# Rotary halves of band attention placed by on-chip transfers instead of a second projection

## The chip, the cores and the metric

The kernel runs on one core of one Trainium2 chip. The metric is device time in microseconds (us) of one execution. TensorE (PE) multiplies matrices, VectorE (DVE), ScalarE (ACT) and GpSimd (POOL) work on vectors, and SyncE (SP) issues transfers (DMAs). Each engine works through its own queue in order and waits on semaphores for the others. SBUF is the on-chip memory; PSUM holds the results of TensorE.

## The reference

Sixteen sequences `b` of 256 tokens and 128 features pass four attentions and three kinds of step between them, all with residual additions. Only the first attention ("band") and what touches it are changed. For one sequence it computes, with 16 heads of 64 features:

```
x0 = layernorm(x[b])                       # 256 x 128
q = rope(x0 @ Wq.T + bq)                   # 16 heads x 64; k the same with Wk, bk
v = x0 @ Wv.T + bv
rope(y): y*cos + concat(-y2, y1)*sin       # y1, y2: the two halves (32 each) of a head's 64 features
scores = q k^T / 8, causal with a band of 128 tokens; p = softmax(scores)
x[b] += (p @ v) @ Wo.T + bo
```

After it come a SwiGLU feed-forward with integer weights (ffn0), a causal attention with 16 heads of 8 features, ffn0 again, a chunked attention, a feed-forward with four-bit quantised operands (ffn1), a low-rank attention, and ffn1 again. Since the rows of `p` sum to one, the value bias adds the constant row `bv @ Wo.T + bo` to the output of the band attention, and a similar row to that of the low-rank attention.

## The kernel before

All of `x` stays in SBUF. The work is 80 units: band, causal, chunk, lowrank and end, each for the 16 sequences. A unit's steps are: forward (the feed-forward ahead of its attention: `xn`, `xT`, `low`, `ffn`, `hid`, for ffn1 also `xq`, `quant`), finish (`down`, `res`), operands (`xn`, `xT`, `low`, `qk`, `cast`, `v`, for the small heads also `rope`, `stack`), maxima (`score`, `parts`), back (`nm`, `S`, `V`) and tail (`den`, `rden`, `scale` or `ctx`, `ctxT`, then `out`). Steps of several units are interleaved.

The order on each engine is set by a planner (`make_plan`, `queued`) before the kernel is built. It walks a model of the five engines with a table of step durations (`work`), waits (`needs`), a settling time after a step (`SETTLE`), and a table of head starts for each engine, stage and kind (`LEAD`). It also assigns every PE result to one of three PSUM slots of 1024 floats; a slot is taken again only when the step named by `released_by` has read it.

Band operands: for each of 8 chunks of 128 features (two heads), `qk` fills a slot with four 128x256 products: queries, queries with the two halves of every head swapped, keys, keys swapped. Weights and tokens are each split into two terms, so a product takes three matmuls (`mm_split`) and a chunk twelve. DVE adds the bias and multiplies by cosine or sine (four instructions, L1178), POOL adds the two parts into `band_r` (L906), and ACT makes a bf16 copy `band_rb` (L927) for the scores that give the row maxima. `nm` carries the maxima to PE, `S` recomputes the scores in f32 with the maxima subtracted, ACT takes the exponential, `V` multiplies by the values.

Small attentions go through a `stack` step: SP writes `parts` to a scratch tensor in HBM with six DMAs (L839, L842) and reads it back into `band_r` memory with four (L851). The planner counts 3.2 us of SP for it and 4.0 us until it has landed.

`out` of band and lowrank ends each of its two token tiles with a matmul of one row of ones by the constant row. In the preamble, `band_qk` is loaded and split in two halves `a` and `b`, the second at the end of it (L663, L697, L698).

## Time and profile before

| | |
|---|---|
| median of 3 runs | 2307.32 us (2299.85 to 2311.41) |
| the profiled execution | 2302.39 us, of which 2300.6 us span |
| PE / DVE busy | 1884.8 us (82%) / 1554.9 us (68%) |
| ACT / POOL busy | 801.2 us (35%) / 594.2 us (26%) |
| mean granted PE clock | 0.892 |

"Busy" is time with an instruction in work; a wait is idle time in front of an instruction. The granted clock is a share of full speed: 1.0 is 2.4 GHz and 0.5 is 1.2 GHz. The program reads as stages: preamble to 50 us, band to about 870 us, causal to 1350, chunk to about 1700, low-rank to 2187, and the end.

### The profile page before, as it was taken

The page shows a single profiled execution, that of the slowest core. Times are in us where ns is not written, and L with a number is a line of the kernel's source. Part 1 is how long each engine was busy: PE and PEld are TensorE (multiplying, and loading weights), DVE is VectorE, ACT ScalarE, POOL GpSimd, SP SyncE. Part 2 cuts the span into 40 slices and gives each one's busy share as a digit, 9 for nine tenths or more (in the row PEclk, how much of TensorE's full clock was granted, in tenths as well). Part 3 has the DMA queues.
Part 4 walks back from the last instruction along what each step waited for, and adds up shares of the span by engine and source line. Part 5 has one row for each costly group of instructions (what it writes and reads, how often), then busy time and mean ns, then how long its engine had stood idle before and what let it go on. Part 6 is the DMA issues. An engine that isn't in the chain of part 4 may idle for free. (4 is left out here: it accounts for less than half of the span.)

```text
span 2300.6 us, 51723 instructions
## 1 busy us (share of the span) xinstructions
PE 1884.8 (82%) x21385; PEld 1280.5 (56%) x21385; DVE 1554.9 (68%) x3419; ACT 801.2 (35%) x1298; POOL 594.2 (26%) x561
## 2 busy tenths in 40 slices
PE   3899999999999998788888888787767877778785
PEld 2566666666666656354455456676644544445454
DVE  5745555554545546566666667888888888887874
ACT  0333333333333332243344343433333434344342
POOL 1322222222222202011111111224433434333334
PEclk7999999999999999899999998877778878787786
DMA  4000000000000001222222224333212211122110
GB/s 150 1 1 1 1 1 1 1 1 1 1 2 1 1 1 29 70 49 55 55 66 64 48 62 91 88 98 91 65 45 53 42 42 42 44 63 45 41 32 10
DMA packets 167464, 89.54 MB, mean 39 GB/s; under 512 B 9393, under 2 KB 165810, under 8 KB 166978
## 3 DMA queue, kind: packets, MB, share of 16 engines
q1 hardware_dynamic: 167010, 85.70, 15.7%
q8 instruction: 173, 2.83, 0.5%
q0 software_dynamic: 224, 0.54, 0.1%
q14 instruction: 57, 0.47, 0.1%
HBM read 46.36 MB, written 39.85 MB: 37 GB/s over the span
## 5 line engine op out<-in xcount | busy, mean ns | idle before, releaser
L1252 PE MATMUL slots<-band_r 64*64 64x64 bf16 (+4 forms) x5120 | 420.9, 280 | 108.6 <-DVE nmx L1135 61.6
L1007 ACT ACTIVATE probs<-slots 128x1024 f32<-128x1024 f32 (+1 forms) x416 | 357.4, 891 | 413.0 <-PE slots L1252 409.4
L1135 DVE TENSOR_REDUCE nmx<-slots 128x8 f32<-128x1024 f32 (+2 forms) x352 | 407.6, 1214 | 102.6 <-PE slots L1252 102.3
L1252 PEld LDWEIGHTS slots<-band_r 64*128 64x128 bf16 (+2 forms) x5120 | 201.0, 129 | 311.0 <-issue 138.3
L1178 DVE SCALAR_TENSOR_TENSOR rope_part<-slots,bias_qk,rope_band 128x256 f32<-128x256 f32 x512 | 212.5, 478 | 195.3 <-PE slots L1252 171.1
L1252 PE MATMUL slots<-mask,ident_bf 128*128 128x256 bf16 (+1 forms) x896 | 230.0, 340 | 75.7 <-DMA band_r<-scratch 50.2
L1252 PE MATMUL ctx_ps<-probs,band_va 64*32 64x64 f32 (+4 forms) x5120 | 253.7, 326 | 16.0 <-ACT ctxT L927 10.7
L906 POOL TENSOR_TENSOR band_r<-rope_part 128x512 f32<-128x512 f32 x128 | 164.8, 1287 | 275.4 <-DVE rope_part L1178 275.4
L864 POOL TENSOR_TENSOR rstd<-var_eps,minus_half 128x2 f32<-128x2 f32 x128 | 88.7, 697 | 544.8 <-DVE var_eps L1048 541.5
L1252 PE MATMUL slots<-nmT,pick 64*128 64x256 bf16 (+2 forms) x2560 | 219.6, 244 | 0.1
L1252 PE MATMUL slots<-xT,band_qk 128*128 128x256 f32 x1536 | 201.1, 288 | 7.6 <-DVEq L1184 5.4
L1252 PEld LDWEIGHTS slots<-xT,band_qk 128*128 128x128 f32 x1536 | 190.0, 191 | 18.2 <-DVEq L1184 12.2
L1252 PEld LDWEIGHTS ctx_ps<-probs,band_va 128*32 128x32 f32 (+2 forms) x5120 | 145.8, 124 | 93.3 <-issue 25.7
L911 POOL TENSOR_TENSOR small_d<-rope_part,parts 128x512 f32<-128x512 f32 x48 | 55.6, 1159 | 474.0 <-ACT parts L927 473.9
L1252 PEld LDWEIGHTS slots<-mask,ident_bf 128*128 128x128 bf16 x896 | 54.5, 98 | 165.3 <-issue 109.3
L927 ACT ACTIVATE ctxT<-ctx_ps 128x512 f32<-128x512 f32 (+1 forms) x112 | 87.5, 781 | 153.0 <-PE ctx_ps L1252 153.0
L927 ACT ACTIVATE band_rb<-band_r 128x512 bf16<-128x512 f32 x128 | 79.4, 630 | 158.8 <-POOL band_r L906 158.8
L1102 DVE SCALAR_TENSOR_TENSOR rope_part<-band_va,slots 128x352 f32<-128x352 f32 (+2 forms) x128 | 68.4, 535 | 62.2 <-ACT band_va L943 30.9
L1252 PEld LDWEIGHTS slots<-nmT,pick 64*128 64x128 bf16 (+1 forms) x2560 | 103.0, 108 | 9.9 <-issue 2.2
L927 ACT ACTIVATE band_va<-slots 128x256 f32<-128x256 f32 (+1 forms) x80 | 50.7, 637 | 133.7 <-PE slots L1252 133.6
L613 POOL TENSOR_TENSOR band_rb<-band_rb 128x704 f32<-128x704 f32 x32 | 53.9, 1686 | 166.5 <-DVEq L1113 166.5
L1527 PE MATMUL slots<-ident,ctxT 128*128 128x128 f32 x384 | 65.2, 301 | 31.1 <-ACT probs L1007 8.4
(171 smaller groups left out, 2871.4 us busy)
## 6 DMA issues: line engine op xcount, KB each, us to landing
band_r<-scratch SPq DMA_DIRECT2D x192, 192.0 KB
scratch<-parts SPq DMA_DIRECT2D x96, 192.0 KB, 2.2
scratch<-parts SPq DMA_DIRECT2D x96, 128.0 KB, 2.1
scratch<-parts SPq DMA_DIRECT2D x96, 64.0 KB, 1.8
x<-in_x SPq DMA_DIRECT2D x16, 128.0 KB, 2.6
out<-x SPq DMA_DIRECT2D x16, 128.0 KB, 1.8
band_r<-in_band_qk_a SPq DMA_DIRECT2D x1, 1024.0 KB, 6.4
band_r<-in_band_qk_b SPq DMA_DIRECT2D x1, 1024.0 KB, 8.1
```

The source lines that it names most:

```text
L613: lambda: v.tensor_tensor(qx, qx, qp, ALU.add),
L864: nc.gpsimd.tensor_tensor(rstd[:, b], var_eps[:, b], minus_half[:], ALU.pow).then_inc(rstd_ready, 1)
L906: nc.gpsimd.tensor_tensor(band_r[:, b % RING, j], part[:, 0], part[:, 1], ALU.add).then_inc(band_sum, 1)
L911: nc.gpsimd.tensor_tensor(small_d[:], small_r, parts[:, 0], ALU.subtract).then_inc(rest1, 1)
L927: return nc.scalar.activation(dst, src, ACT.Copy)
L1007: nc.scalar.activation(probs[:, g % 2, step[2], :, 0:width], slot(u, step).rearrange("p (a n) -> p a n", a=2)[:, :, 0:width], ACT.Exp, sca ...
L1102: link(nc.vector.scalar_tensor_tensor(g_out, t_in, 1.0, gate, ALU.add, ALU.mult))
L1135: nc.vector.tensor_reduce(dst, src, axis=AX.X, op=ALU.max, negate=True).then_inc(free_sem(u, step), 1)
L1178: nc.vector.scalar_tensor_tensor(rope_part[:, c % 2, rot, qk, :], slot(u, step)[:, o:o + TOK], bias_qk[:, j, 2 * qk + rot:2 * qk + rot + 1 ...
L1252: return nc.tensor.matmul(o, lhsT, rhs, start=start, stop=stop, skip_group_check=shared)
L1527: last = nc.tensor.transpose(B[:, g * P:(g + 1) * P], ctxT[:, g, t * P:(t + 1) * P], ident[:])
```

## The change

1. Band weights are regrouped. A fill now holds four heads (a "quad"): first halves of queries and keys, then second halves, four heads of 32 features on the 128 partitions. There are 4 fills for each sequence instead of 8, and nothing is projected twice.
2. DVE still runs 32 multiplications for a sequence: step `qk` makes the first rotated half (first half by cosine, second by sine), step `rot` the second. A slot is held until `rot` is done. POOL subtracts or adds into a new buffer `quad_r` (two quads deep).
3. SP then copies `quad_r` into `band_r` with four transfers of 32 partitions x 512 floats (64 KB) after `qk` and four after `rot`: 32 for a sequence. ACT waits for them (`band_moved`) and casts two chunks at a time (4 casts of 128x1024 instead of 8 of 128x512).
4. The constants of band and lowrank are added to `x` by POOL (step `bias`, 128x256, 32 times), and the two matmuls in `out` go. `out` on DVE waits for `bias`.
5. The preamble loads and splits `band_qk` once at half the total size, and spreads the two constant rows over 128 partitions with two matmuls and two copies.
6. The planner's numbers change: `stack` 7.6 us of SP and 4.3 us to land, settling times for SP by step, all head starts, and the term for the unit's number. So the order changes in every stage.

```
-        for j in range(CHUNKS + CAST_LAG):
-            if j < CHUNKS:
-                steps.append(("qk", j))
-            if j >= CAST_LAG:
-                steps.append(("cast", j - CAST_LAG))
+        for m in range(QUADS + CAST_LAG):
+            if m < QUADS:
+                steps += [("qk", m), ("rot", m)]
+            if m >= CAST_LAG:
+                steps.append(("cast", m - CAST_LAG))
...
-        "stack": [("sp", 3.2)],
+        "stack": [("sp", 7.6)],
...
-SETTLE = {"pe": 0.18, "act": 0.12, "dve": 0.1, "pool": 0.08, "sp": 4.0}
+SETTLE = {"pe": 0.18, "act": 0.12, "dve": 0.1, "pool": 0.08}
+LANDS = {"stack": 4.3, "qk": 1.7, "rot": 1.7, "res": 1.4}
...
-        "operands": {"band": 19.904, "causal": 0.469, "chunk": 0.14, "lowrank": 3.336},
+        "operands": {"band": 0.166, "causal": -0.064, "chunk": 3.447, "lowrank": 12.532},
...
+    if name == "qk":
+        return u, ("rope",) if small else ("rot", step[1]), "dve"
...
+                    if kind == "band" and step[0] in ("qk", "rot"):
+                        m, second = step[1], step[0] == "rot"
+                        quad = b * QUADS + m
+                        sp.wait_ge(band_sum, 2 * quad + second + 1)
+                        if b >= RING and step == ("qk", 0):
+                            sp.wait_ge(back_full, last_exp(u - RING) + 1)
+                        for i in range(4):
+                            to = 64 * (i % 2) + 32 * second
+                            sp.dma_start(band_r[to:to + 32, b % RING, 2 * m + i // 2],
+                                         quad_r[32 * i:32 * i + 32, quad % 2, second]).then_inc(band_moved[quad % 2], 16)
...
+                    if step == ("bias",):
+                        pool.wait_ge(xn_ready, XN_NO[u, False] + 1)
+                        nc.gpsimd.tensor_tensor(x[:, b], x[:, b], const[kind][:].unsqueeze(1).to_broadcast([P, TILES, DIM]),
+                                                ALU.add).then_inc(const_added, 1)
...
+                        quad, second = b * QUADS + step[1], step[0] == "rot"
+                        n = 2 * quad + second
                         pool.wait_ge(part_ready, 4 * (n + 1))
-                        if b >= RING and j == 0:
-                            pool.wait_ge(back_full, last_exp(u - RING) + 1)
+                        if quad >= 2:
+                            pool.wait_ge(band_moved[quad % 2], 128 * (quad // 2))
...
-                        act.wait_ge(band_sum, b * CHUNKS + j + 1)
+                        act.wait_ge(band_moved[quad % 2], 128 * (quad // 2 + 1))
...
-                            if has_const:
-                                last = mm(o, ones[:], const_row[kind][:], False, True)
```

The order on DVE, in the middle of the band stage, for one sequence. Before, all eight chunks stand together (`rope_part`), after `out` of an earlier sequence:

```order
L1230 TENSOR_TENSOR ctxT<-slots,ctxT 128x512 x4
L1242 TENSOR_TENSOR x<-slots,x 128x256
L1045 BN_STATS stats<-x 128x6 x2
L1047 BN_AGGR mean_var<-stats 128x2 x2
L1048 TENSOR_SCALAR var_eps<-mean_var 128x2
L1178 SCALAR_TENSOR_TENSOR rope_part<-slots,bias_qk,rope_band 128x256 x32
```

The same place now: three quads (24 multiplications), then `qk` and `rot` of the fourth between the maxima (`nmx`) of the sequence before and the `scale` steps (`ctxT`):

```order
L1215 SCALAR_TENSOR_TENSOR rope_part<-slots,bias_qk,rope_band 128x256 x24
L1171 TENSOR_REDUCE nmx<-slots 128x2x4 x2
L1215 SCALAR_TENSOR_TENSOR rope_part<-slots,bias_qk,rope_band 128x256 x4
L1171 TENSOR_REDUCE nmx<-slots 128x2x2
L1261 RECIPROCAL rden<-slots 128x2x4x4
...
L1268 TENSOR_TENSOR ctxT<-slots,ctxT 128x512 x4
L1171 TENSOR_REDUCE nmx<-slots 128x2x2
L1215 SCALAR_TENSOR_TENSOR rope_part<-slots,bias_qk,rope_band 128x256 x4
L1171 TENSOR_REDUCE nmx<-slots 128x2x2
```

So the fourth quad's slot is held through most of the pass over the maxima.

The order on ACT at the start of a back half, before: the copy of the maxima (`nmT`) follows the copies of the values (`band_va`) and `xT`, and the casts (`band_rb`) are spread among the copies of `ctxT`:

```order
L927 ACTIVATE band_rb<-band_r 128x512 x5
L927 ACTIVATE ctxT<-ctx_ps 128x512
L927 ACTIVATE band_rb<-band_r 128x512 x2
L927 ACTIVATE ctxT<-ctx_ps 128x512
L927 ACTIVATE den_sb<-ctx_ps 128x256
L927 ACTIVATE band_rb<-band_r 128x512
L927 ACTIVATE band_va<-slots 128x1024 x2
L927 ACTIVATE xT<-slots 128x256
L927 ACTIVATE nmT<-slots 128x256
```

And now, with all four casts right ahead of `nmT`, which stands behind the last transfer of the fourth quad:

```order
L962 ACTIVATE ctxT<-ctx_ps 128x512 x2
L962 ACTIVATE den_sb<-ctx_ps 128x256
L962 ACTIVATE rdT<-slots 128x256
L962 ACTIVATE band_rb<-band_r 128x1024 x4
L962 ACTIVATE nmT<-slots 128x256
L962 ACTIVATE band_va<-slots 128x1024 x2
L1043 ACTIVATE probs<-slots 128x1024
```

The order on PE in the causal stage. The projection `xT,causal_qkv` feeds the stack of its sequence; the rows `mask` and `band_r 128x128 x8` begin the pass over the maxima. Before, the projection comes after that pass, and its own scores follow a little less than one period later:

```order
L1252 MATMUL slots<-mask,ident_bf 128x512 x2
L1252 MATMUL slots<-band_r 128x128 x8
L1252 MATMUL slots<-mask,ident_bf 128x512 x2
L1252 MATMUL slots<-band_r 128x128 x8
L1252 MATMUL slots<-mask,ident_bf 128x2x128 x2
L1252 MATMUL slots<-band_r 128x256 x4
...
L1252 MATMUL slots<-xT,causal_qkv 128x256 x12
L1252 MATMUL slots<-mask,ident_bf 128x2x128 x2
L1252 MATMUL slots<-band_r 128x256 x2
```

Now it comes ahead of the pass of the sequence before it, so that its own scores follow more than one period later:

```order
L1292 MATMUL slots<-xT,causal_qkv 128x256 x12
L1292 MATMUL slots<-mask,ident_bf 128x256 x2
...
L1567 MATMUL slots<-ident,ctxT 128x128 x4
L1292 MATMUL slots<-mask,ident_bf 128x512 x2
L1292 MATMUL slots<-band_r 128x128 x8
L1292 MATMUL slots<-mask,ident_bf 128x512 x2
L1292 MATMUL slots<-band_r 128x128 x8
```

The projection moved from behind the pass to ahead of it.

## Rows read from the trace of the kernel before

**Rows 1.** Windows by stage: length, busy us per engine, granted clock, DMA.
```profile
112.00:870.00 758.00, 711.13 (x6524) 485.38 (x6520) 404.31 (x935) 245.51 (x382) 164.41 (x141) 1.00 0.01 1
1003.00:1350.00 347.00, 286.97 (x3027) 171.29 (x3026) 226.47 (x492) 132.00 (x223) 44.95 (x51) 0.92 0.24 56
...
1723.00:2187.00 464.00, 353.64 (x3120) 225.54 (x3120) 389.21 (x792) 186.83 (x290) 178.54 (x167) 0.81 0.21 47
2187.00:2301.00 114.00, 78.23 (x624) 55.55 (x622) 70.53 (x156) 37.93 (x61) 45.78 (x39) 0.75 0.08 18
```
**Rows 2.** Timeline of PE over one band sequence: start, us.
```profile
407.53 0.29 PE L1485 MATMUL slots<-ident_bf,nm 128*128 128x128 bf16 x2
...
416.80 0.48 PE L1252 MATMUL slots<-const_band,ones 1*128 1x128 f32 x2
...
422.98 0.61 PE L1252 MATMUL slots<-mask,ident_bf 128*128 128x512 bf16 x2
...
425.94 1.52 PE L1252 MATMUL ctx_ps<-probs,band_va 128*64 128x256 f32 x16
...
431.13 9.02 PE L1252 MATMUL slots<-xT,band_qk 128*128 128x256 f32 x72
...
442.21 1.70 PE L1252 MATMUL slots<-xT,band_qk 128*128 128x256 f32 x12 [0.18 <-DVEq L1184]
443.84 1.52 PE L1252 MATMUL ctx_ps<-probs,band_va 128*64 128x256 f32 x16
...
459.19 0.28 PE L1485 MATMUL slots<-ident_bf,nm 128*128 128x128 bf16 x2
```
**Rows 3.** Timeline of DVE over the same sequence.
```profile
400.07 6.88 DVE L1135 TENSOR_REDUCE nmx<-slots 128x8 f32<-128x1024 f32 x6 [0.99 <-PE slots L1252]
...
411.65 2.48 DVE L1230 TENSOR_TENSOR ctxT<-slots,ctxT 128x512 f32<-128x512 f32 x4 [1.71 <-PE slots L1252]
...
432.94 1.66 DVE L1178 SCALAR_TENSOR_TENSOR rope_part<-slots,bias_qk,rope_band 128x256 f32<-128x256 f32 x4 [11.51 <-PE slots L1252]
434.81 1.66 DVE L1178 SCALAR_TENSOR_TENSOR rope_part<-slots,bias_qk,rope_band 128x256 f32<-128x256 f32 x4 [0.21 <-DVE rope_part L1178]
...
450.01 0.73 DVE L1061 TENSOR_SCALAR xn<-x,mean_var,rstd 128x128 f32<-128x128 f32 x2 [0.89 <-POOL rstd L864]
```
**Rows 4.** Page, costliest groups: line, operation, count, busy, mean ns, idle before.
```profile
L906 POOL TENSOR_TENSOR band_r<-rope_part 128x512 f32<-128x512 f32 x128 | 164.8, 1287 | 275.4 <-DVE rope_part L1178 275.4
```
**Rows 5.** Timeline of SP's queue in the causal stage.
```profile
1038.19 2.52 SPq L851 DMA_DIRECT2D band_r<-scratch  x4
```
**Rows 6.** Page, DMA issues: count, size each, us to landing.
```profile
scratch<-parts SPq DMA_DIRECT2D x96, 64.0 KB, 1.8
```
**Rows 7.** Waits of PE in 860:1000, 1000:1340, 1340:1590: total, times, longest.
```profile
PE slots L1252 <- DMA band_r<-scratch: 10.7, 3, 4.9
...
PE slots L1252 <- DMA band_r<-scratch: 39.5, 12, 4.3
...
PE slots L1252 <- DMA band_r<-scratch: 4.3, 2, 2.6
```
**Rows 8.** Timeline of PE at one of these waits.
```profile
1044.95 0.62 PE L1252 MATMUL slots<-mask,ident_bf 128*128 128x512 bf16 x2 [4.05 <-DMA band_r<-scratch]
```
**Rows 9.** Windows of 2 us around it: length, PE busy, granted clock, DMA.
```profile
1042.00:1044.00 2.00, 0.00 (x0) 1.00 0.88 137
...
1046.00:1048.00 2.00, 2.00 (x15) 0.50 0.00 0
```
**Rows 10.** Timeline of DVE at the end of the preamble.
```profile
36.91 1.23 DVE L697 CAST band_qk<-band_r 128x2048 fp32r<-128x2048 f32 x1
38.17 2.29 DVE L698 TENSOR_TENSOR band_qk<-band_r,band_qk 128x2048 fp32r<-128x2048 f32 x1
```
**Rows 11.** Timeline of POOL in the last 30 us.
```profile
2270.86 1.68 POOL L613 TENSOR_TENSOR band_rb<-band_rb 128x704 f32<-128x704 f32 x1 [2.75 <-DVEq L1113]
...
2285.98 1.67 POOL L613 TENSOR_TENSOR band_rb<-band_rb 128x704 f32<-128x704 f32 x1 [10.21 <-DVEq L1113]
```

More of the change, by code:

```diff
@@ L40 @@
 QUANT_OPS = (range(0, 3), range(3, 6), range(6, 9))
+QUADS = HEADS // 4
 CAST_LAG = 2
@@ L220, in needs @@
             yield u - 1, ("nm",), "pe"
+        if name == "out" and kind in CONSTANT:
+            yield u, ("bias",), "pool"
     if eng == "act":
@@ L242, in needs @@
     if eng == "pool":
+        if name == "bias":
+            yield u, ("xn", False), "dve"
         if step == ("xq", 1):
@@ L308, in released_by, with settles @@
+        "forward": {"lowrank": -1.38, "end": -7.778},
+        "operands": {"band": -33.144, "causal": -56.912, "chunk": 76.381, "lowrank": -16.786},
+    },
+}
+PER_UNIT = 0.0038
+def settles(step, eng):
+    return LANDS[step[0]] if eng == "sp" else SETTLE[eng]
 def released_by(u, step):
```

174 lines of the change are left out of this document (90 added, 84 removed).

## The prediction

> **What bounds the kernel now.** I read the windows by stage first [rows 1]. In the band stage (112 to 870 us) PE is busy 711 of 758 us, 93.8%, at full clock; DVE works 53% of it. So there PE's work is the time, and what leaves PE there pays. In the causal stage PE is busy 83% and DVE 65%, and the mean clock is 0.92: neither fills it. In the low-rank stage DVE is busy 389 of 464 us, 84%, and leads. In the last 114 us both are low (PE 69%, DVE 62%).
>
> The timeline of PE then gives the band period: `nm` to `nm` is 459.19 - 407.53 = 51.66 us [rows 2]. The eight `qk` fills stand together from 431.13 to 443.84, 12.71 us, with two 0.18 us waits for DVE among them [rows 2].
>
> The waits of PE show what the causal stage lacks: 10.7 + 39.5 + 4.3 = 54.5 us in 17 waits for `band_r<-scratch`, the read-back of `stack`, almost one for each causal sequence [rows 7]. One of them, 4.05 us [rows 8], leaves PE without work in 1042 to 1044; the granted clock is 1.00 up to there and 0.50 (1.2 GHz) in 1046 to 1048, while PE is busy throughout [rows 9]. So such a wait costs more than its own length.
>
> **Part 1: projection.** Half of the 96 matmuls go: 12.71 / 2 = 6.36 us for a sequence [rows 2]. The two constant matmuls go too, each 0.48 us [rows 2] with some overlap: 0.9. On a path held by PE that leaves 51.66 - 6.36 - 0.9 = 44.4 us, waits of before included. PE's idle share was 6.2%, or 3.2 us, so PE's own work is then about 51.66 - 3.2 - 6.2 (the 6.36 less one of the two waits) - 0.9 = 41.3; the walk below adds 40.5 of named steps.
>
> **Part 2: the new band order.** DVE's work is unchanged (32 multiplications), but a slot is now held until `rot`, and the fourth quad's is held through the pass over the maxima. I walk one sequence, in us.
>
> First part, from the first score fill to `nm`. PE's own work is 15.5: six scores at about 0.86, one `V` 2.24 (I take `S` at 1.8 wide and 1.1 narrow from the same rows: a wide and a narrow `S` fill 422.98 to 425.94, 2.96 [rows 2]), `out` 4.0, small fills 0.9, two `v` 3.2. DVE has to do, in order: two maxima at 6.88 / 6 = 1.15, `qk` 1.87 (434.81 - 432.94), one maximum, `den` 1.2, one maximum, four `scale` 2.48, one maximum, `rot` 1.87, the last maximum, `parts` 0.9 [rows 3]. That is 15.2, beginning 0.9 after PE. With two free slots only, `scale` waits for DVE's chain: fills for the last two scores come at 10.3 and, behind `out`, at 15.2. `v` is done at 19.3, so `nm` starts at 19.3: 3.8 of wait.
>
> Second part. DVE still has `out` with its statistics (1.7), the statistics of the next sequence (1.3), POOL's root (0.9 of wait) and `xn` 0.73 [rows 3], so `xT` on PE can't start before 3.5 after `nm`; PE meanwhile has `nm` and one wide `S`, 2.0, and a wait of 0.5 for ACT. Three `qk` fills take all slots; the next `S` waits 0.5 for the first `rot`. Together 2.2 of wait on 25.0 of work. Sum: 19.3 + 27.2 = 46.5.
>
> The transfers end in the same place. The fourth `rot` leaves DVE at 14.3; POOL's addition takes 1.29 [rows 4]; four transfers are issued in 2.5 (four take 2.52 [rows 5]); the last lands 1.8 later (64 KB [rows 6]): 19.9, and the cast ends at about 21. `nm`'s copy on ACT is queued behind it, with both `v` copies and the exponentials behind that, so `S` starts 1.2 later; most of this lies in the wait for `xT`, and 0.2 is left. I take **46.7**: 51.66 - 46.7 = 5.0 for each of 16 sequences, **-80 us**. Bounds: no added wait at all (44.4) gives -116; for the transfers the nearest other row is the stack's read-back, whose scores begin 4.2 us after its last issue (1044.95 against 1038.19 + 2.52 [rows 5, 8]), 2.4 more than I used, which gives 49.1 and -41. SP issues 32 x 0.63 = 20 us for a sequence, under half of the period, so the queue keeps up if transfers overlap.
>
> The row for a 64 KB transfer is 1.8 us, between HBM and 128 partitions [rows 6]; none shows 32 partitions. The Trainium skill (SBUF — State Buffer, "Door 1: The DMA port swizzle") says that partitions 0 to 31 reach 8 of the 16 ports, at about 218 GB/s against 436, and advises 128 partitions and large transfers. By it 64 KB cost 0.15 us more, an estimate, and the period would be 46.8. No run here shows this, and neither figure changes the sum.
>
> **Part 3: `bias`.** 32 additions on POOL of half the size of its band addition, 1.29 / 2 = 0.65 us each [rows 4]. POOL is busy 22% in the band stage [rows 1] and the result is wanted by `out`, tens of us later: 0. If POOL held up the first rotated quad, it would be 0.65 x 16 = 10; the removed matmuls in low-rank (0.9 x 16 = 14 on PE) lie beside DVE, which leads there: 0, at best -14.
>
> **Part 4: preamble.** The second split, 1.23 + 2.29 = 3.5 us [rows 10], stands last there and goes. The constant's spreading overlaps the quantised weights' work: **-3.5**, between -3.5 and -1.
>
> **Part 5: the order of the later stages.** Work stays the same but all head starts differ. In the causal stage the projection moves ahead of the previous sequence's pass, so the distance to its own scores grows from less than a period to more than one. It gains at least the pass it is moved past and itself, 6 x 0.86 + 1.6 = 6.8 us; the waits are at most 4.9 [rows 7]. They should go: **-54.5**. Who is late next: PE, or DVE at 65%. The window holds twelve sequences (it runs from the first DMA of one stack to that of the twelfth after it), 28.9 us each, of which PE idles 5.0 [rows 1]; 39.5 / 12 = 3.3 of these are the waits. Bounds: the waits only change name, 0; or they take the half-clock stretches with them: 8% of 347 us is lost to the clock [rows 1], another -28, plus -29 at the end, where five instead of seven ffn1 quantisations are left behind the last low-rank cast, 15.1 us apart (2285.98 - 2270.86 [rows 11]). I leave both out: 6 more feed-forwards now run around the end of band and cost time there, and the ffn1 work moved into the chunk stage fills it.
>
> The Trainium skill (TensorE: Matmul & The Clock Gate, "HAM oscillation — how this bites in real kernels") says that a matmul burst after a DMA wait starts at half clock each time. The trace agrees: 0.50 after 4.05 us [rows 8, 9]. It would speak for the lower bound.
>
> **Sum.** The profiled execution took 2302.4 us (span 2300.6), 4.9 less than the median of 2307.3. 2302.4 - 80 - 3.5 - 54.5 = **2164 us**.
>
> **Rivals.**
> - *Band pays, later stages don't.* DVE or PE takes over the 54.5 us of waits, or the earlier feed-forwards cost them back. For it: DVE already leads in low-rank, 84% [rows 1]. Against: 35% of idle on DVE in causal. 2302.4 - 83.5 = 2219.
> - *Band pays less.* The casts hold ACT, and with it `nm` and `S`, by 2.4 more, as worked out: 2164 + 39 = 2203. The same size results if the 4 us or so without steady work around `nm` brings the half clock for 5 us of each sequence: 2.5 x 16 = 40. Against: 6% of idle left the clock at 1.00 in band before [rows 1].
> - *More than forecast.* The half-clock stretches and the end as above: 2164 - 28 - 29 = 2107.
> - *Slower: the moves run one behind the other.* If a transfer between partitions doesn't overlap the next, a sequence needs 32 x 1.8 = 58 us of them [rows 6] against a period of 51.66; with the later gains that is 2302.4 + 16 x 6 - 58 = 2340. It decides from 2302.4 + 16(32t - 51.66) - 58 = 2302, a transfer time t of 1.73 us. Against: four read-backs of 192 KB, three times the size, are there 1044.95 - 1038.19 = 6.8 us after the first issue [rows 5, 8], less than four times 1.8 in a row.
>
> **How the numbers follow.** Forecast 0.52, of itself 2125 to 2195; band alone 0.14; band less 0.11; more 0.16; slower 0.04; no change, by several smaller losses, 0.03. The range of 2095 to 2225 takes in the three rivals around the forecast. Below 0.5% (about 11 us) a time can't be told from no change here. Faster is 0.93, same 0.03, slower 0.04.
>
> **What would show it.** Band period: 46 to 48 us from `nm` to `nm`, 48 projections in each, PE busy about 88% and still at clock 1.0. Waits of PE for DVE's `nmx` or `xT` near `nm`, and for ACT's `nmT`. Transfers `band_r<-quad_r`: 512, landing near 2 us, issued about 0.6 apart. No or few waits of PE for `band_r<-scratch`, and a causal period under 27 us instead of 28.9. Wrong would be: transfers landing after 4 us or more, clock below 0.95 in band, or a span from the last band exponential to the end as long as before (about 1430 us).

## The result

The changed kernel takes 2299.3 us (median of 20, 2291.8 to 2308.9) against 2306.0 for the kernel before on the same chip (20 runs, 2295.9 to 2317.2): a ratio of 0.9969, interval 0.9954 to 0.9984. The forecast was 2164. A gain of 7 us is left of 138.

The profiled execution takes 2297.8 us, its span is 2295.9. PE is busy 1795.3 us instead of 1884.8. That is 90 us less, where the prediction takes 16 x 7.26 = 116 out of band alone; part of what is left ran at half clock. DVE is busy 1609.8 instead of 1554.9, with no less and no more to compute. The windows by stage of the changed kernel, answering to [rows 1] (its low-rank stage begins later):

```profile
112.00:870.00 758.00, 647.05 (x5796) 412.59 (x5795) 414.53 (x932) 235.26 (x330) 170.22 (x152) 0.91 0.16 40
1003.00:1350.00 347.00, 314.29 (x3436) 191.90 (x3435) 250.71 (x558) 147.97 (x248) 50.65 (x56) 0.98 0.24 62
1774.00:2187.00 413.00, 313.81 (x3040) 210.50 (x3040) 361.38 (x661) 183.46 (x275) 149.57 (x143) 0.86 0.22 56
2187.00:2295.00 108.00, 64.75 (x548) 46.84 (x544) 71.75 (x131) 32.70 (x50) 31.86 (x29) 0.74 0.06 14
```

In the band window PE is busy 64 us less, but its clock is 0.91 where it was 1.00. To see where the time went I cut every trace at the same marks, the starts of the `nm` fills on PE (u is a band sequence, "causal" runs from the `nm` of its first sequence to that of chunk's first). The two left columns add up to the two spans; the others are kernels of the experiments. The period repeats within 0.01 us and the first two rows within 0.6 in two kernels with the same band (deep4 and pool_twice, below). The later rows are less sure: the profiled execution of deep4 is 12 us below that kernel's median, that of bias_only 7 above, and chunk reads 385.8, 387.9 and 391.7 in three kernels with the same order there. A difference of a few us in these rows says nothing.

| us | before | changed | before_late | bias_only | deep4 | pairs | qk2_s31 |
|---|---|---|---|---|---|---|---|
| to `nm` of u0 | 104.1 | 105.3 | 104.0 | 104.1 | 103.4 | 96.6 | 96.5 |
| u0 to u1 | 45.1 | 60.6 | 45.1 | 45.1 | 60.7 | 55.4 | 54.7 |
| u1 to u14, each of 13 | 51.66 | 50.88 | 51.66 | 50.49 | 48.61 | 48.60 | 47.79 |
| u14 to u15 | 28.8 | 32.2 | 28.8 | 27.7 | 32.3 | 32.3 | 32.3 |
| u15 to causal | 77.4 | 107.6 | 104.4 | 72.6 | 107.2 | 107.3 | 107.5 |
| causal | 454.1 | 413.5 | 418.4 | 461.2 | 412.7 | 412.7 | 412.8 |
| chunk | 329.0 | 391.7 | 399.8 | 342.1 | 385.8 | 387.9 | 391.7 |
| low-rank | 525.6 | 463.4 | 483.2 | 526.4 | 458.4 | 461.7 | 461.5 |
| last `nm` to the end | 65.0 | 60.1 | 60.4 | 63.2 | 59.2 | 59.2 | 59.1 |

So the start lost 15.5 us, 13 periods gained 10.1 where 64.5 were forecast (13 x 4.96), and all behind band gained 11.4 net (1479.9 to 1468.5 from the `nm` of u14 on, 3.4 of loss in u14 to u15 included).

The 13 periods in one window each, before, changed and deep4 (the changed kernel with two buffers more, below):

```profile
149.19:820.74 671.55, 630.70 (x5771) 430.72 (x5771) 365.00 (x839) 217.40 (x338) 151.28 (x129) 1.00 0.01 1
165.90:827.40 661.50, 569.46 (x5097) 365.21 (x5096) 372.74 (x846) 205.57 (x287) 159.33 (x143) 0.92 0.17 42
164.14:796.03 631.89, 561.11 (x5097) 363.31 (x5096) 363.04 (x846) 205.37 (x287) 159.80 (x143) 0.95 0.18 44
```

For each period PE is busy 48.5, 43.8 and 43.2 us and idle 3.1, 7.1 and 5.4. The forecast of 46.7 was 41.3 of work and 5.4 of idle. So the changed kernel has 2.5 us more of work than forecast, on a clock of 0.92, and 1.7 more of idle.

**One band sequence after.** The timeline of PE, around the place that [rows 2] show:

```profile
397.99 0.61 PE L1292 MATMUL slots<-mask,ident_bf 128*128 128x512 bf16 x2
...
406.26 1.03 PE L1292 MATMUL slots<-mask,ident_bf 128*128 128x512 bf16 x2 [2.74 <-DVE nmx L1171]
408.59 0.37 PE L1525 MATMUL slots<-ident_bf,rd 128*128 128x128 bf16 x2 [0.76 <-DVE rd L1182]
...
413.42 4.87 PE L1292 MATMUL slots<-band_o,ctxT 128*128 128x128 f32 x32
...
421.87 0.29 PE L1525 MATMUL slots<-ident_bf,nm 128*128 128x128 bf16 x2
...
449.69 0.61 PE L1292 MATMUL slots<-mask,ident_bf 128*128 128x512 bf16 x2
```

From the first score fill (397.99) to `nm` are 23.9 us, where the walk had 19.3; from `nm` to the next first score fill 27.8, where it had 27.2. The loss is in the first part. Follow the 2.74 us back: DVE's maximum was late because the `qk` step of the fourth quad ahead of it had waited for POOL, and POOL had waited for a transfer. POOL, DVE and SP's queue at that time:

```profile
386.00 1.27 POOL L940 TENSOR_TENSOR quad_r<-rope_part 128x512 f32<-128x512 f32 x1 [0.29 <-DVE rope_part L1215]
402.11 2.49 POOL L940 TENSOR_TENSOR quad_r<-rope_part 128x512 f32<-128x512 f32 x2 [14.85 <-DMA band_r<-quad_r]
406.64 1.26 POOL L940 TENSOR_TENSOR quad_r<-rope_part 128x512 f32<-128x512 f32 x1 [2.04 <-DMA band_r<-quad_r]
```
```profile
403.42 1.66 DVE L1215 SCALAR_TENSOR_TENSOR rope_part<-slots,bias_qk,rope_band 128x256 f32<-128x256 f32 x4 [2.10 <-POOL quad_r L940]
...
406.73 1.22 DVE L1180 TENSOR_TENSOR nmx_r<-rden,rd 128x32 f32<-128x32 f32 x1
```
```profile
394.27 7.06 SPq L858 DMA_DIRECT2D band_r<-quad_r  x10
```

The transfer itself is quick to land, as the page's part on DMA has it (answering to [rows 6]):

```profile
band_r<-quad_r SPq DMA_DIRECT2D x512, 64.0 KB, 2.0
```

What held it is what SP waited for between 200 and 750 us (total, times, longest):

```profile
SPq L855 <- PE slots L1292: 261.7, 10, 26.9
```

L855 is SP's wait for the last `S` of the sequence two before: `band_r` has two entries, and the first quad's transfers overwrite the one which that `S` still reads. The new order puts three `qk` fills of u ahead of `S:1,1` to `S:3,1` of u - 2. Their sums come in 380.99 to 387.27, `quad_r` holds two quads, and nothing leaves until 394.27. Then the sixteen transfers of these two quads are issued in a row, 0.7 us each.

The windows of 2 us show the second price. PE has no work in 404 to 406, and then runs at 1.2 GHz for 10 us:

```profile
404.00:406.00 2.00, 0.00 (x0) 0.00 (x0) 2.00 (x4) 0.00 (x0) 0.61 (x1) 0.84 0.45 113
406.00:408.00 2.00, 1.57 (x6) 0.26 (x6) 1.90 (x5) 0.00 (x0) 1.26 (x1) 0.50 0.40 101
...
412.00:414.00 2.00, 2.00 (x8) 0.76 (x9) 0.92 (x2) 0.00 (x0) 0.00 (x0) 0.50 0.39 98
414.00:416.00 2.00, 2.00 (x13) 2.00 (x13) 2.00 (x5) 0.00 (x0) 0.00 (x0) 0.60 0.00 0
```

`band_o` takes 4.87 us here; at full clock its two groups take 2.05 each.

### The profile page after: what moved, and what is told of

Read it like the earlier page. It is cut to its first block and busy times, and to the rows that moved or that the text cites. A ratio compares the mean times of both kernels' runs of the same rounds, so it can differ in the third digit from the quotient of the medians.

```text
span 2295.9 us, 50383 instructions
## 1 busy us (share of the span) xinstructions
PE 1795.3 (78%) x20493; PEld 1228.5 (54%) x20493; DVE 1609.8 (70%) x3419; ACT 787.6 (34%) x1234; POOL 615.8 (27%) x593
## 5 line engine op out<-in xcount | busy, mean ns | idle before, releaser
L1171 DVE TENSOR_REDUCE nmx<-slots 128x8 f32<-128x1024 f32 (+2 forms) x352 | 415.3, 1217 | 235.6 <-PE slots L1292 231.3
L1292 PE MATMUL slots<-band_r 64*64 64x64 bf16 (+4 forms) x5120 | 400.6, 272 | 93.1 <-DVE band_r L1139 44.2
L940 POOL TENSOR_TENSOR quad_r<-rope_part 128x512 f32<-128x512 f32 x128 | 162.3, 1274 | 490.3 <-DVE rope_part L1215 246.6
L1292 PE MATMUL ctx_ps<-probs,band_va 64*32 64x64 f32 (+4 forms) x5120 | 262.6, 327 | 27.3 <-issue 16.4
L1215 DVE SCALAR_TENSOR_TENSOR rope_part<-slots,bias_qk,rope_band 128x256 f32<-128x256 f32 x512 | 207.6, 476 | 66.7 <-PE slots L1292 37.5
L1292 PEld LDWEIGHTS ctx_ps<-probs,band_va 128*32 128x32 f32 (+2 forms) x5120 | 148.3, 125 | 107.8 <-issue 58.1
L962 ACT ACTIVATE band_rb<-band_r 128x1024 bf16<-128x1024 f32 x64 | 63.0, 1047 | 195.4 <-PE slots L1292 140.1
L1292 PE MATMUL slots<-xT,band_qk 128*128 128x256 f32 x768 | 103.3, 292 | 3.8 <-DVE xT L1114 3.7
L1292 PEld LDWEIGHTS slots<-xT,band_qk 128*128 128x128 f32 x768 | 96.9, 194 | 11.3 <-issue 9.7
L1097 DVE TENSOR_SCALAR band_va<-x,mean_var,rstd 128x128 f32<-128x128 f32 x128 | 91.7, 717 | 6.4 <-POOL rstd L894 1.7
L1292 PE MATMUL slots<-fp_gu,xTf 128*128 128x352 f32 x384 | 75.1, 348 | 17.3 <-DVE xTf L1114 16.9
L1081 DVE BATCH_NORM_STATS2 stats<-x 128x6 f32<-128x128 f32 x256 | 75.2, 294 | 13.1 <-DMA x<-in_x 4.6
```

The source lines that it names most:

```text
L940: nc.gpsimd.tensor_tensor(quad_r[:, quad % 2, second], part[:, 0], part[:, 1], ALU.add if second else ALU.subtract).then_inc(band_sum, 1)
L962: return nc.scalar.activation(dst, src, ACT.Copy)
L1081: link(nc.vector.bn_stats(stats6[:, t, :], x[:, b, t, :]))
L1097: last = nc.vector.tensor_scalar(xn[:, t, :], x[:, b, t, :], mean_var[:, b, t, 0:1], rstd[:, b, t:t + 1], ALU.subtract, ALU.mult)
L1171: nc.vector.tensor_reduce(dst, src, axis=AX.X, op=ALU.max, negate=True).then_inc(free_sem(u, step), 1)
L1215: nc.vector.scalar_tensor_tensor(rope_part[:, c % 2, sine, qk, :], slot(u, ("qk", m))[:, at * TOK:(at + 1) * TOK], bias_qk[:, m, at:at + 1 ...
```

## The experiments

All ratios are to the kernel before, which ran beside each.

### Is it the wait for `band_r`?

**deep4**: four rotated sums may lie waiting, not two; the order is untouched.

```diff
-        quad_r = sb("quad_r", [P, 2, 2, 2, TOK])
+        quad_r = sb("quad_r", [P, QBUF, 2, 2, TOK])      # QBUF = 4, as the band_moved semaphores
-                        if quad >= 2:
-                            pool.wait_ge(band_moved[quad % 2], 128 * (quad // 2))
+                        if quad >= QBUF:
+                            pool.wait_ge(band_moved[quad % QBUF], 128 * (quad // QBUF))
```

> The changed kernel with four rotated-sum buffers (quad_r) instead of two; the order of the work is the same. Theory (the ring wait): in the changed kernel the transfers of a sequence's first quad wait on SP's queue for the last S of the sequence two before, whose copy of band_r they overwrite; two quads of sums fill quad_r, GpSimd then waits 14.9 us for a transfer, DVE 2.1 us and TensorE 2.7 us behind it, and the granted clock is 0.50 for the next 9 us. With four buffers GpSimd's wait goes below 2 us, the clock of that place is back near 1.00, the row max nmx_r beside the add is near 0.2 us again instead of 1.22, and the band's period falls from 50.9 us to 46.5 to 48; 14 periods of 3 to 4.4 us are 40 to 60 us: 2240 to 2258 us, 0.972 to 0.980 of the kernel before. Rival one (the clock and the waits come from the order of the fills, not from the buffers): period 50 to 51, 2290 to 2300 us. Rival two (the wait only moves to the casts on ACT, since band_r is still two sequences deep): GpSimd is free, but a TensorE wait for the cast of 2 us or more appears and the period is 49 to 50: 2272 to 2285 us.

Measured: 0.982 (0.979 to 0.985), 2265.9 us, 34 less than the changed kernel. POOL waits for no transfer any more, SP waits as before (286.5 us in 11 waits), and `nmx_r` takes 0.19. The wait is shown to be the cause of 2.3 us a period, 30 of the 34. But the period is 48.6, not 46.5 to 48, and the time lies between the theory's range and that of its second rival. From `nm` (406.92) to the first score fill (434.74) are 27.8 us, as before; the rest is 21.7, and the half clock is still in it, later. (The period shown is one of the long ones, 49.5.) PE's timeline and one window of 2 us of deep4:

```profile
439.86 0.41 PE L1547 MATMUL slots<-ident,den_sb 128*128 128x128 f32 x2 [0.22 <-ACT den_sb L963]
440.96 0.61 PE L1293 MATMUL slots<-mask,ident_bf 128*128 128x512 bf16 x2 [0.69 <-DVE nmx L1172]
...
446.87 6.00 PE L1293 MATMUL slots<-band_o,ctxT 128*128 128x128 f32 x32
...
456.46 0.29 PE L1526 MATMUL slots<-ident_bf,nm 128*128 128x128 bf16 x2
```
```profile
440.00:442.00 2.00, 1.20 (x8) 0.26 (x7) 1.86 (x6) 0.00 (x0) 0.98 (x1) 1.00 0.39 98
```

The granted clock puts a price on it. Six of deep4's 13 periods hold 6.8 us at 1.2 GHz and take 49.2 us on average, the other seven hold 3.4 us and take 48.1: 1.0 us for 3.4 us of half clock.

**late_qk**: the same wait removed by order; the planner gets back the rule of the kernel before.

```diff
+        if kind == "band" and step == ("qk", 0) and u >= RING:
+            yield u - RING, LAST_S["band"], "pe"
```

> The changed kernel with one rule added to the order's planner, the one that the kernel before had: the first fill of a sequence's quads stands behind the last S of the sequence two before on TensorE. The buffers are as in the changed kernel. Theory (the ring wait): SP's wait for band_r before the first quad's transfers is then over when they are issued, GpSimd's 14.9 us wait for a transfer goes below 3 us, the granted clock stays near 1.00 there, and the period falls from 50.9 to between 47 and 49.5 (not the full 4.4, since the fills now come later and their sums reach the casts later): 2260 to 2285 us. Rival (the order of the fills costs by itself what it saves, or the two buffers hold GpSimd in either order): period 50 to 52, 2290 to 2310 us.

Measured: 1.042 (1.039 to 1.045), 2401 us, period 58.1. Both ranges missed it. POOL's waits for a transfer did go (16.6 us in 10 waits between 200 and 750), but SP now stands still for POOL's sums (156.3 us in 39 waits), PE waits for ACT's `band_va` copies (26.3 us in 9 waits, none in deep4), and 13.7 us of each period run at half clock. The wait can be bought off with a buffer and not with this order.

### What do the later stages' orders give?

**before_late**: the kernel before with the changed head starts (`LEAD`) of the later stages, the planner's costs and landing times of SP's steps and `PER_UNIT`. PE's order behind band then differs from the changed kernel's in 40 of 1376 steps.

```diff
-PER_UNIT = 0.0005
+PER_UNIT = 0.0038
-        "forward": {"causal": -0.243, "chunk": 0.183, "lowrank": 0.15, "end": -0.153},
+        "forward": {"causal": 9.367, "chunk": -0.061, "lowrank": 27.724, "end": 0.591},
...
-        "stack": [("sp", 3.2)],
+        "stack": [("sp", 7.6)],
```

> The kernel before, with only the head starts and the stack's planned cost that set the order of the causal, chunk, low-rank and last stages taken from the changed kernel; the band's code and order stay those of before. By the account of the two traces the later stages together give 15 to 20 us (causal 35.5 less, chunk 92 more, low-rank 90 less, between band and causal 17.6 more): 2286 to 2292 us, 0.992 to 0.995 of before. By the prediction's fifth part they give 54.5 us: 2250 us. Rival: the gain needs the new band's free DMA queues or ACT, and here nothing or less than nothing is left: 2302 to 2315 us.

Measured: 1.0058 (1.0038 to 1.0078), 14 us slower; the rival held in kind, 3 us beyond its range. In the table causal gives 35.7, and 27 are lost ahead of it, 71 in chunk, 42 come back in low-rank, 4.6 at the end. PE's waits for the read-back, 50.2 us in causal before, are gone. In their place DVE is busy longer. The windows behind the `nm` of u14 in one line each, before and before_late:

```profile
sum 1479.86, PE 1154.76 PEld 780.51 DVE 1091.49 ACT 550.24 POOL 403.91; mean PE 230.95 PEld 156.10 DVE 218.30 ACT 110.05 POOL 80.78
```
```profile
sum 1495.06, PE 1161.87 PEld 821.56 DVE 1145.31 ACT 551.49 POOL 405.13; mean PE 232.37 PEld 164.31 DVE 229.06 ACT 110.30 POOL 81.03
```

54 us more of DVE at the same work. By form, mainly two operations of both traces (count, busy, mean ns), before and then before_late:

```profile
L1061 DVE TENSOR_SCALAR band_va<-x,mean_var,rstd 128x128 f32<-128x128 f32 x128 | 65.2, 509 | 18.2 <-PE ctx_ps L1252 15.1 <-POOL rstd L864 0.8
L1202 DVE TENSOR_TENSOR rope_part<-rope_part,small_d 128x512 f32<-128x512 f32 x32 | 22.1, 692 | 4.7
```
```profile
L1062 DVE TENSOR_SCALAR band_va<-x,mean_var,rstd 128x128 f32<-128x128 f32 x127 | 91.3, 719 | 6.3 <-POOL rstd L865 1.7 <-DVE band_rb L613 0.3
L1203 DVE TENSOR_TENSOR rope_part<-rope_part,small_d 128x512 f32<-128x512 f32 x32 | 37.6, 1174 | 5.4 <-DVE small_d L1201 1.0
```

One of them in before_late's chunk stage, with what POOL does then:

```profile
1478.88 2.10 DVE L1203 TENSOR_TENSOR rope_part<-rope_part,small_d 128x512 f32<-128x512 f32 x1
1480.91 2.51 DVE L1062 TENSOR_SCALAR xn<-x,mean_var,rstd 128x128 f32<-128x128 f32 x2
```
```profile
1478.75 1.69 POOL L615 TENSOR_TENSOR band_rb<-band_rb 128x704 f32<-128x704 f32 x1
1480.52 1.71 POOL L616 TENSOR_TENSOR band_r<-band_rb 128x704 f32<-128x704 f32 x1
```

An addition of 0.69 us takes 2.10 when it begins just behind one of POOL's: POOL's ends at 1480.44, and DVE's 0.54 later. The Trainium skill (SBUF — State Buffer, "Who interferes with whom") says that a VectorE instruction with two inputs in SBUF, or in one of its two-port modes, and a GpSimd one share a port that the first holds to its end. The trace agrees here, and with `nmx_r` above, 1.22 us beside POOL's sum and 0.19 without. Summed over both traces behind the `nm` of u14, against the median of the same form where no operation of POOL overlaps it: DVE's operations with inputs in SBUF alone lost 52 us beside POOL in before and 103 in before_late, those that read PSUM within 1 us of nothing beside POOL. So 51 of the 54 us are this.

**pool_twice** tests that. It is deep4, and the last multiplication of each quantisation is done twice.

```diff
+                if v is nc.gpsimd and i == 8:
+                    link(ops[i]())
                 last = ops[i]()
```

> The kernel deep4 (0.982 of before, DVE busy 1597 us) in which GpSimd does the last multiplication of each ffn1 quantisation twice (the same values into the same place): 32 x 1.7 and 32 x 0.6 us, 74 us more of GpSimd's work in the causal, chunk and low-rank stages, where it is busy about a third of the time. Theory (an operation of DVE whose inputs are both in SBUF stands still while one of GpSimd runs, and so the late stages' 54 us of DVE time come from where GpSimd's work stands, not from more work): DVE's busy time grows by 15 to 50 us with no instruction added to it, and the time by 15 to 40 us: 2281 to 2306 us. Rival (GpSimd is off the path and does not touch DVE): DVE's busy time within 3 us of 1597, the time at most 10 us longer, by the last multiplication's consumers: 2266 to 2276 us.

Measured: 0.9983 (0.9966 to 1.0001), 2299.6 us: 34 more than deep4 for 65 us more of POOL, and DVE busy 24 us more (1621.0) without an instruction more of its own. Both numbers are in the theory's range. PE's waits for POOL grew by 10 us too, so the 34 are not DVE's alone; that POOL's work costs time in these stages, though it was busy 40% of them or less, is shown.

**after_oldlate**: the changed kernel with the head starts and SP's planned costs of before for the later stages.

```diff
-        "forward": {"causal": 9.367, "chunk": -0.061, "lowrank": 27.724, "end": 0.591},
+        "forward": {"causal": -0.243, "chunk": 0.183, "lowrank": 0.15, "end": -0.153},
```

> The changed kernel, with the head starts and the stack's planned cost of the later stages taken back to those of before; the band's code and order stay those of the changed kernel. If the later order gives 15 to 20 us, this one takes 2312 to 2320 us, about 1.003 to 1.007 of before, and the band's code alone is then a small loss (its start 15.5 us dearer, 13 periods 10.1 us cheaper). By the prediction's fifth part it would be 54.5 us above the changed kernel: 2350 us. Rival: chunk's loss of 92 us goes while causal's gain of 35 us stays, and the time falls below 2290 us.

Measured: 1.0568 (1.054 to 1.0595), 2435 us. It misses every expectation, and says little: with the band's steps ahead of them the planner puts the feed-forwards one or two sequences away from where they stood in the kernel before, so this isn't its order. It shows only that such a table holds for one program.

### What are the constants worth?

**peconst** is deep4 with the constants added by PE again, **bias_only** the kernel before with them added by POOL. Orders are kept. The core of peconst, and what bias_only puts in POOL's step of a band sequence:

```diff
-                                last = mm(o, src, w, j == 0, j == chunks - 1)
+                                last = mm(o, src, w, j == 0, j == chunks - 1 and kind not in CONSTANT)
+                            if kind in CONSTANT:
+                                last = mm(o, ones[:], const_row[CONSTANT.index(kind)][:], False, True)
```
```diff
+                    pool.wait_ge(xn_ready, XN_NO[u, False] + 1)
+                    nc.gpsimd.tensor_tensor(x[:, b], x[:, b], const[kind][:].unsqueeze(1).to_broadcast([P, TILES, DIM]),
+                                            ALU.add).then_inc(const_added, 1)
```

> The kernel deep4 with the constants of the band and low-rank outputs added by TensorE again (two matmuls of 1 x 128 by 128 for a sequence) and GpSimd's 32 additions left out; the order of all other work is the same. The prediction gave the moved constants 0.9 us of TensorE for a band sequence and nothing for a low-rank one, at best 14 us: then this kernel takes 14 us more than deep4, 2280 us, 0.988 of before, and the low-rank stage is within 3 us of deep4's. Theory from the traces: before_late and the changed kernel have nearly the same order in the low-rank stage and differ by 20 us there, 1.24 us for each sequence, of which these matmuls are the main difference; then this kernel takes 14 + 20 more: 2300 us, 0.997 of before. Rival: GpSimd's additions cost DVE as much as the matmuls cost TensorE, and the time is that of deep4, 2263 to 2270 us.

> The kernel before with one part of the change alone: the constants of the band and low-rank outputs are added to x by 32 additions on GpSimd, and the matmuls that added them (two of 1 x 128 by 128 for each sequence) are gone; projection, casts and order are those of before. By the prediction's terms: 16 x 0.9 = 14 us in the band, low-rank 0, so 2291 us, 0.994 of before. By what peconst measured on top of deep4 (54 us, 31 in the band, 22 in the last stages): 2250 us, 0.977. In between would be: in this kernel the band's clock is 1.00, so that only the matmuls' own 0.9 us count there, while the low-rank stage gives its 22 us: 2265 to 2272 us, 0.984. If it is below the changed kernel (0.997), then the halved projection with its transfers is a loss by itself.

Measured: peconst 1.0069 (1.0055 to 1.0083), 2319.6 us, 54 more than deep4, beyond all that was expected (63 between the two profiles: 2.1 for each of 13 periods, 22 in low-rank, 14 in all other parts). Its periods hold 7.3 us at half clock on average, those of deep4 5.0. bias_only 0.9957 (0.994 to 0.9973), 2293.5 us. There a period gives 1.17, near the 0.9 of the forecast, low-rank gives nothing, and causal and chunk are 20 us longer in that profile. So the same two matmuls cost 9 us in one kernel and 54 in the other; why low-rank differs is open. And bias_only is no slower than the whole change: with two buffers, the halved projection, its transfers and the later stages' new order together were worth nothing in time. No run has the halved projection with the old order behind it, so these three are not told apart.

### What do the transfers cost at the start?

**pairs**: deep4, with the weight columns laid so that two heads' halves go in one transfer, 64 source partitions to 32, 128 KB.

```diff
-                        for i in range(4):
-                            to = 64 * (i % 2) + 32 * second
-                            sp.dma_start(band_r[to:to + 32, b % RING, 2 * m + i // 2],
-                                         quad_r[32 * i:32 * i + 32, quad % QBUF, second]).then_inc(band_moved[quad % QBUF], 16)
+                        for i in range(2):
+                            to = 64 * i + 32 * second
+                            sp.dma_start(band_r[to:to + 32, b % RING, 2 * m:2 * m + 2],
+                                         quad_r[64 * i:64 * i + 64, quad % QBUF, second]).then_inc(band_moved[quad % QBUF], 16)
```

> The kernel deep4 (0.982 of before) with half as many transfers in the band: the weight columns of a quad are laid so that two heads' halves go in one transfer of 64 source partitions to 32 target partitions, 128 KB, 16 for a sequence instead of 32. Theory (SP's issue time sets the start): in deep4 the casts of the first two sequences follow each other every 5.07 us, which is eight issues of 0.63 us; TensorE waits 9.3 us for ACT behind them at 76.3 and 6.5 us at 117.2. With four issues for a quad 2.5 us each go, so the distance from the first nm to the second falls from 60.7 to 50 to 53 us and the first nm comes 5 to 8 us sooner; in the steady part nothing changes (48.6 us). Together 13 to 20 us: 2246 to 2253 us, 0.974 to 0.977 of before. Rival (an issue costs by its bytes, or the landing grows from 2.0 to 4 us or more, so that the pace of the casts stays 5 us): 2262 to 2270 us.

Measured: 0.9778 (0.9756 to 0.980), 2251.9 us, 14 less than deep4. The theory holds, though the second step is smaller than said: 6.8 us at the first `nm`, 5.3 to the second instead of 8 or more, nothing in the steady part. In the changed kernel and in pairs, two casts of ACT that follow each other at the start:

```profile
64.22 1.06 ACT L962 ACTIVATE band_rb<-band_r 128x1024 bf16<-128x1024 f32 x1 [4.02 <-DMA band_r<-quad_r]
69.29 1.06 ACT L962 ACTIVATE band_rb<-band_r 128x1024 bf16<-128x1024 f32 x1 [4.01 <-DMA band_r<-quad_r]
```
```profile
60.73 1.06 ACT L963 ACTIVATE band_rb<-band_r 128x1024 bf16<-128x1024 f32 x1 [2.35 <-DMA band_r<-quad_r]
64.18 1.06 ACT L963 ACTIVATE band_rb<-band_r 128x1024 bf16<-128x1024 f32 x1 [2.39 <-DMA band_r<-quad_r]
```

5.07 us and 3.45 us apart: eight issues of 0.63, four of 0.86. (In the first 10 us of the two queues they are 9.49 / 15 and 9.61 / 12, 0.63 and 0.80.) The larger transfer lands in 3.1 us instead of 2.0.

### What keeps the period at 48.6?

Four kernels move one thing among the scores or fill a wait there. **late_scale** (on deep4) holds `scale` and `out` back; **qk3_den**, **qk2_v2** and **qk2_s31** (on pairs) put a `qk` fill elsewhere. Each is a rule in the planner's `needs`:

```diff
late_scale: +        if name == "scale" and kind == "band" and u + 1 < BATCH:
            +            yield u + 1, ("S", 0, 1), "pe"
qk3_den:    +        if kind == "band" and step == ("qk", 3) and u >= RING:
            +            yield u - RING, ("den",), "pe"
qk2_v2:     +        ... step == ("qk", 2) ...:  yield u - RING, ("V", 2), "pe"
qk2_s31:    +        ... step == ("qk", 2) ...:  yield u - RING, ("S", 3, 1), "pe"
```

> The kernel deep4 with one rule more in the planner of the order: a band sequence's four scale fills, and with them its out, stand behind the next sequence's second S fill, as they did in the kernel before, and no longer among its score fills. In deep4 the granted clock still falls to 0.50 for 6 us in each sequence, after 5 us in which TensorE, waiting in short pieces for the chain rden, rdT, scale, is busy only 55 to 65%. Theory (that chain makes the half clock): TensorE's work among the scores is then denser, the clock stays at 1.00 and the period falls from 48.6 to 46 to 47.5 us: 14 x 1.1 to 2.6 = 15 to 36 us less, 2230 to 2251 us. Rival (the same short waits come back in the S pass, where DVE and ACT are late): the clock falls there instead, period 48 to 50, 2260 to 2285 us.

> The kernel pairs with its fourth qk fill moved behind den, so that TensorE has 1.7 us of projection just where it waited in short pieces ahead of rd and scale. Theory (the half clock comes from TensorE's low share of work there, 0.76 and 1.31 us busy in two stretches of 2 us): the clock stays at 1.00, band_o takes 4.0 us again instead of 6.0, and the period falls from 48.3 to 46 to 47.3 us: 2230 to 2246 us. Rival (the fourth quad's rot now comes behind scale on DVE, its cast is late, nm and S wait for it): period 49 or more, above 2262 us.

> The kernel pairs (0.978 of before) with the third and fourth qk fill of a sequence put behind the third V of the sequence two before, next to each other and just ahead of the last V; the score fills move behind the scale fills accordingly. The later stages keep their order. Theory (the first part is paced by DVE's own list of maxima, rot and scale while TensorE waits in short pieces and its clock falls): here TensorE has 3 us of projection ahead of the chain den, rden, scale, but rot work of two quads stands right beside it on DVE. If the half clock goes, the period falls from 48.3 to 46 to 47.5 us: 2233 to 2250 us. Rival (DVE is late with the two rots and the casts are late for the first score): period 49 to 52, 2265 to 2305 us.

> The kernel pairs with its third qk fill moved from ahead of the S pass to its end, where it stands directly ahead of the fourth. The wait of the fourth S for the first rot shrinks, and DVE, which waits 9.6 us at the end of the S pass, has a quad to work on; the chain den, rden, scale and its half clock stay as they are. Expected: 0.3 to 1 us less for each period (47.3 to 48.0 us), 2238 to 2248 us. Rival: the casts, which follow the last score of the sequence before, are late with the third quad and period and time stay within 3 us of pairs, 2249 to 2255 us.

| | ratio (interval) | us | period |
|---|---|---|---|
| late_scale | 1.0161 (1.0144 to 1.0178) | 2342.6 | 54.5 |
| qk3_den | 1.0142 (1.0117 to 1.0167) | 2335.1 | 54.7 |
| qk2_v2 | 0.9811 (0.9791 to 0.9831) | 2260.2 | 49.2 |
| qk2_s31 | 0.9733 (0.9712 to 0.9753) | 2241.7 | 47.8 |

In the first three the rival's sign held, in late_scale by far more than it gave (period 48 to 50), in qk3_den within a range that had no upper end, in qk2_v2 with the period at its lower edge and the time 5 us below it. The first two have a wait of PE that deep4 and pairs don't have, for ACT's `band_va` copies (28.7 and 14.1 us in 10 waits each between 200 and 750), and 10.7 and 13.7 us of half clock in a period. qk2_s31 came as expected and is the best kernel of the study, 61 us below the one before (2302.8 beside it). The waits for the first `rot` (`DVEq`, 6.8 us in 12 between 200 and 750 in pairs) are gone. Its clock still falls, for 5.5 us a period on average.

**warm** gives PE idle work in qk2_s31 where it waits for `rd` and `rdT`.

```diff
+                def idle_work(B, times):
+                    for _ in range(times):
+                        mm(B[:, 0:512].rearrange("p (h w) -> p h w", w=256), ident_bf[:],
+                           mask[:, 0:256].unsqueeze(1).to_broadcast([P, 2, 256]))
...
                     if name == "rden":
+                        idle_work(B, 1)
...
                         if g == 0:
+                            idle_work(B, 2)
```

> The kernel qk2_s31 (0.973 of before, period 47.8 us) with idle work on TensorE: one matmul of 512 columns written into the slot of rden before its wait, two into the slot of the first scale before its wait for rdT; the real fills overwrite them. In the trace of qk2_s31 TensorE waits 0.37 and 0.56 us there, the last part of 6 us in which it is busy about 55%, and the matmuls of band_o behind it take 5.2 us, in deep4 6.0, instead of the 4.0 that the two groups of them took at full clock in the kernel before. Theory (the fall to 1.2 GHz comes from TensorE's low share of work in these 6 us): with 0.9 us more of work there the clock stays up or falls later, band_o takes 4.0 to 4.5 us, the period falls by 0.7 to 1.5 us: 2220 to 2232 us. Rival (the clock falls all the same, and the idle work only delays the chain by up to 0.3 us): 2241 to 2250 us.

Measured: 0.9746 (0.9723 to 0.9769), 2245.1 us, period 47.8: no gain, in the rival's range. The windows at the same place, and last the 13 periods in one, qk2_s31 and then warm:

```profile
424.00:426.00 2.00, 1.07 (x11) 0.41 (x10) 1.76 (x5) 0.38 (x1) 0.00 (x0) 1.00 0.56 131
426.00:428.00 2.00, 0.79 (x7) 0.31 (x6) 2.00 (x4) 0.00 (x0) 0.00 (x0) 1.00 0.00 0
428.00:430.00 2.00, 2.00 (x11) 1.24 (x10) 1.35 (x2) 0.00 (x0) 0.00 (x0) 0.59 0.00 0
151.16:772.45 621.29, 558.51 (x5097) 363.70 (x5096) 363.12 (x846) 205.38 (x287) 159.68 (x143) 0.94 0.22 45
```
```profile
424.00:426.00 2.00, 1.40 (x9) 0.34 (x8) 1.45 (x3) 0.38 (x1) 0.00 (x0) 1.00 0.57 131
426.00:428.00 2.00, 0.82 (x5) 0.32 (x6) 2.00 (x4) 0.00 (x0) 0.00 (x0) 0.87 0.00 0
428.00:430.00 2.00, 2.00 (x9) 0.88 (x8) 0.92 (x2) 0.00 (x0) 0.00 (x0) 0.50 0.03 8
150.60:772.00 621.40, 561.38 (x5137) 358.55 (x5137) 363.24 (x846) 205.39 (x287) 159.67 (x143) 0.96 0.22 45
```

PE had more to do, and the clock at this place fell sooner and not later. `band_o` was 0.6 us shorter (4.59), and the steps ahead of it 0.8 longer. Over the 13 periods the half clock did shrink, from 5.5 us a period to 3.4, and the period stayed: 47.79 and 47.80. In qk2_s31 itself periods with 6.8 us of half clock take 47.9 us and those with 3.4 take 47.6. So in this order the half clock is nearly free, a third of its price in deep4. What would hold the clock at this place stays open.

## Why the prediction was wrong

Against the sum: band and preamble were put at -83.5 us and came out at +6.7 (to the `nm` of u14); all behind it was put at -54.5 and came out at -11.4.

- **Part 1, projection: the work was right, the value was not.** 48 projections and the constants' matmuls are gone for each sequence, and PE is busy 43.8 us of a period instead of 48.5. The step "a path held by PE" failed: once the halving was taken off, DVE's, POOL's and SP's turns stood on the path, and PE's idle time in a period rose from 3.1 to 7.1 us.
- **Part 2, the walk, 46.7 us: 50.88 measured.** The failed step is "The transfers end in the same place". I followed the fourth quad to its cast, and asked of SP's queue only whether it keeps up ("under half of the period, so the queue keeps up"). The diff gives SP a wait, L855, and I didn't ask what is queued behind it: sixteen transfers, two buffers, POOL, DVE, the scores. deep4 puts 2.3 us of the 4.2 on it. In deep4 PE idles 5.4 us of a period, as forecast; the other 1.9 are work that took longer (43.2 instead of 41.3), most of it `out` at half clock (6.00 us instead of 4.0 in the period shown). That the half clock makes these 1.9 is worked out and not shown by a run: by the price above its 5.0 us a period would be 1.5. I had priced the half clock in a rival, at 40 us and a chance of 0.11 shared with the casts, and argued against it from PE's 6% of idle. That idle was an average; after the change it is 5 us in one place. Its 2.5 us a period are what PE's work exceeds the forecast by in the changed kernel, but that rival came together with the wait, not alone.
- **The start wasn't in the sum.** I took 5.0 off "each of 16 sequences". The first one had nothing to hide its transfers behind: the distance to the second grew by 15.5, which pairs shortens by the issues it leaves out. Nor does the first `nm` come 3.5 us sooner (part 4); it comes 1.3 later, for the same cause.
- **Part 3, constants: mis-sized.** 0.9 us a sequence was 1.17 in the kernel before and 2.1 in deep4; low-rank, put at 0 "beside DVE, which leads there", gave 22 in deep4 and nothing in bias_only. It is the one part of the change that paid by itself in both kernels where it was tried.
- **Part 5, later stages: -54.5 forecast, about -11 measured, the moved constants included.** The waits for the read-back did go. Between 850 and 1600 us the changed kernel has, answering to [rows 7],

```profile
PE slots L1292 <- DMA band_r<-scratch: 0.6, 1, 0.6
```

  and PE is busy 91% of the causal window instead of 83%, at 0.98. What failed is "they should go" taken for time. I named DVE as next, at 65%, and left it at that; the feed-forwards moved cost 30 us ahead of causal, and DVE got 54 us longer beside POOL. In before_late the new order loses 14 us by itself. (The bound of -29 at the end, left out of the sum, would be 2 x 15.1 = 30 by its own rows.)
- **The range** ended at 2225, the rival "Band pays, later stages don't" at 2219. No rival with a time of its own had both parts fail; "no change, by several smaller losses", which is what happened, had a chance of 0.03. The rival that ended slower (moves one behind the other) was aimed at the transfers' duration: landing after 2.0 us (1.8 in the sum) and issued 0.6 apart, they were as forecast.

## What to carry to other kernels

When a change hands work to a queue, list that queue's waits in the new order and count how many buffers fill up behind each of them: here two more buffers were worth 34 us, five times the whole change. A wait that leaves is time only if the engine named next isn't already slowed where the work is moved to; take its durations from rows where the neighbours run, too. Count the first and the last turn of a loop apart from the steady ones.

## What the runs showed of the hardware

- A transfer between partitions in SBUF costs SP 0.63 us of issue at 64 KB and 0.80 to 0.86 at 128 KB, landing after 2.0 and 3.1 us; at the start of a program the issue sets the pace.
- The granted clock fell to 1.2 GHz a few us behind a stretch of short waits, none over 0.7 us: PE was busy 3.3 of 6 us in deep4's 440 to 446. In the kernel before it stayed at 1.00 through 458 to 460, with 1.02 us of work in 2. What 3.4 us of half clock cost was 1.0 us of a period in deep4 and 0.3 to 0.4 in qk2_s31.
- Some of DVE's operations with inputs in SBUF alone took longer beside POOL's: in the changed kernel a 128x128 fp32 TENSOR_SCALAR 0.34 us on average with no overlap and 1.46 with one (60 of 256), `nmx_r` 0.19 and 1.22. The multiplications that read PSUM (128x256, L1215) took 0.46 and 0.47.
